# A four-layer graph network on one core: the tie verdict, the refinement loops, the adjacency transfers and the order of the diffusions

## The reference, cut to what matters

```python
def _top_p_attention(X, W1, W2, W3):
    q = X @ W1.T @ W2.T
    k = X @ W3.T
    probs = softmax(q @ k.T, axis=-1)            # 5000 x 5000
    idx = argsort(-probs, axis=-1)
    sp = take_along_axis(probs, idx, axis=-1)
    keep_sorted = cumsum(sp) - sp < 0.9          # top-p: smallest set with 90% of the mass
    A = probs * mask_of(keep_sorted)
    return A / A.sum(-1)
...
R = (adj + eye(N)); R = R / R.sum(-1)
for n in range(2):
    A = _top_p_attention(Xa, W1, W2, W3)
    Xf = R @ Xf                                  # "diffusion"
    Xa = A @ Xa                                  # "attention"
    Z = Z + Xf @ U1[n].T + Xa @ U2[n].T
```

## Time and profile before

| | |
|---|---|
| Time, median of 3 runs | 6468.54 us (6465.03 to 6469.6) |
| The profiled execution | 6475.32 us |
| Its span, from the first to the last instruction | 6473.6 us |
| VectorE busy | 5090.3 us, 79% |
| TensorE busy (matmul) | 4486.8 us, 69% |
| ScalarE busy | 2199.2 us, 34% |
| Mean DMA rate | 84 GB/s |

### The profile page before, as it was taken

The page is one execution under the profiler, slowest core; times in us unless marked ns, Lnnn a source line. Parts: engine busy times, 40 slices in busy tenths (PEclk is TensorE's granted clock), DMA queues, the critical chain, the costliest instruction groups (busy, mean ns, idle before and its releaser), DMA issues. The chain is left out here.

```text
span 6473.6 us, 79162 instructions
## 1 busy us (share of the span) xinstructions
PE 4486.8 (69%) x27812; PEld 3206.8 (50%) x27812; DVE 5090.3 (79%) x12501; ACT 2199.2 (34%) x3353; POOL 327.7 (5%) x170
## 2 busy tenths in 40 slices
PE   6996688888766435452678978575368888847982
PEld 2443377767656335442567867464222222216982
DVE  5887488888518888888888989895649999994875
ACT  2332567666411111111234444233041222214542
POOL 0000000000020000000001000000002022020000
PEclk9997799999889678777889999787689999978996
DMA  8552000000033112111212222112023333314850
GB/s 199 202 200 92 1 2 2 2 2 1 1 115 123 57 53 108 71 72 55 84 72 88 93 80 83 64 64 34 17 70 101 114 111 107 113 35 164 289 189 16
DMA packets 177849, 541.61 MB, mean 84 GB/s; under 512 B 20204, under 2 KB 62303, under 8 KB 177303
## 3 DMA queue, kind: packets, MB, share of 16 engines
q1 hardware_dynamic: 172246, 531.90, 23.7%
q0 software_dynamic: 5120, 3.97, 0.3%
HBM read 524.17 MB, written 11.56 MB: 83 GB/s over the span
## 5 line engine op out<-in xcount | busy, mean ns | idle before, releaser
L680 PE MATMUL ps<-ident,arena 125*125 125x125 f32 x3200 | 539.3, 302 | 863.9 <-DVEq L1186 863.9
L712 PE MATMUL ps<-arena 125*125 125x129 f32 x6400 | 834.5, 289 | 315.3 <-DMA arena<-in_adj_tiles 306.2
L1488 DVE SCALAR_TENSOR_TENSOR arena<-arena,pair 125x1000 f32<-125x1000 f32 x800 | 939.3, 1250 | 69.9 <-ACT arena L1451 69.9
L712 PEld LDWEIGHTS ps<-arena 125*125 125x125 f32 x6400 | 782.3, 199 | 387.1 <-DMA arena<-in_adj_tiles 302.5
L688 PE MATMUL ps<-arena,turned 125*125 125x129 f32 x6400 | 912.3, 290 | 8.0 <-ACT turned L794 8.0
L680 PEld LDWEIGHTS ps<-ident,arena 125*125 125x125 f32 x3200 | 469.5, 215 | 903.8 <-DVEq L1186 903.7
L1506 PE MATMUL ps<-arena 125*64 125x500 f32 x3200 | 763.4, 600 | 194.4 <-DVE arena L1488 194.4
L794 ACT ACTIVATE turned<-ps 125x500 f32<-125x500 f32 x800 | 465.3, 585 | 1268.9 <-PE ps L680 1268.5
L688 PEld LDWEIGHTS ps<-arena,turned 125*125 125x125 f32 x6400 | 838.7, 202 | 19.8 <-ACT turned L794 13.3
L1506 PEld LDWEIGHTS ps<-arena 125*64 125x64 f32 x3200 | 197.4, 137 | 757.4 <-DVE arena L1488 527.3
L1139 DVE SCALAR_TENSOR_TENSOR arena<-arena,wt 125x5000 f32<-125x5000 f32 x80 | 434.1, 5426 | 155.6 <-issue 155.6
(11 more groups left out here) (349 smaller groups left out, 6048.9 us busy)
## 6 DMA issues: line engine op xcount, KB each, us to landing
arena<-in_adj_wide SPq DMA_DIRECT2D x400, 500.0 KB, 4.5
arena<-in_adj_tiles SPq DMA_DIRECT2D x400, 488.3 KB
arena<-in_adj_wide SPq DMA_DIRECT2D x100, 1000.0 KB, 4.7
x_saved<-arena SPq DMA_DIRECT2D x2, 2240.0 KB
arena<-x_saved SPq DMA_DIRECT2D x2, 2240.0 KB
arena<-att_saved SPq DMA_DIRECT2D x1, 2257.5 KB
arena<-in_x SPq DMA_DIRECT2D x1, 2240.0 KB
arena<-in_h SPq DMA_DIRECT2D x1, 2240.0 KB
```

What stands on the lines that cost most here:

```text
L680: mm = pe.transpose(banks_turn[:, g % 2, c * P:(c + 1) * P], work[b % depth][:, j:j + P], ident[0:P, 0:P])
L712: mm = pe.matmul(acc_spread, ring[:, j * P:(j + 1) * P], values[:, j, :], start=(j == 0), stop=False)
L1488: v.scalar_tensor_tensor(out=weight(m).rearrange("p (g w) -> p g w", g=2), in0=rows(ERB + h * N + r * PASS, PASS).rearrange("p (g w) -> p ...
```

## The change

Four things are changed. (a) In `keep`, the drain ahead of the verdict's load goes away; a drain stands inside the branch that needs it. (b) In `refine` both bisection loops are unrolled. (c) In `opened` the nested loops of 4 and 3 rounds give way to one `refine` without a condition, a second under a condition, and under one more a loop of ten; the three are each emitted, so that `opened` holds `refine` three times with its bisections unrolled. (d) The adjacency tiles are laid out with 128 rows for each block, the last three zero, and the ring takes 128 partitions. The order of the diffusions is another: 8, 8, 6, 6, 4, 0, 6, 6 in the first eight blocks, then one in each of 28 blocks, then none. With it `scaled_at` goes from block 9 to block 6.

```diff
-REFINE_ROUNDS = (4, 3)
+REFINE_ROUNDS = 12
-SPREADS = (5, 3, [4] * 8 + [0, 3, 3] + [1, 1, 2, 1] * 6 + [2, 2, 0, 0, 0])
+SPREADS = (5, 3, [8, 8, 6, 6, 4, 0, 6, 6] + [1] * 28 + [0] * 4)
...
-                ring = rows(RING, N)
+                ring, padded_ring = rows(RING, N), rows(RING, N, 128)
...
-                            sp.dma_start(ring[:, q * 1000:(q + 1) * 1000],
-                                         adj_tiles[r * P:(r + 1) * P, q * 1000:(q + 1) * 1000])\
+                            sp.dma_start(padded_ring[:, q * 1000:(q + 1) * 1000],
+                                         adj_tiles[r * 128:(r + 1) * 128, q * 1000:(q + 1) * 1000])\
                               .then_inc(loaded[q], 16)
...
                     def refine(w, cand):
-                        with v.Fori(0, BISECTIONS):
+                        for _ in range(BISECTIONS):
                             bisect(w, dump, goal)
...
-                        with v.Fori(0, CANDIDATE_BISECTIONS):
+                        for _ in range(CANDIDATE_BISECTIONS):
                             bisect(cand, windows, rest)
...
                         v.scalar_tensor_tensor(out=w, in0=w, scalar=found, in1=w, op0=ALU.is_ge, op1=ALU.mult,
                                                accum_out=kept_mass)
-                        v.drain()
                         if rounds > 1:
+                            v.drain()
                             v.match_replace(w, needles[:, 0:8], w, 0.0)
-                            v.drain()
                         ties = worst()
                         with v.If(ties > 0):
+                            v.drain()
                             at = 8 if rounds > 1 else 0
                             v.match_replace(w, needles[:, at:at + 8], w, 0.0)
...
                             mass_above(cand, windows, hi, base)
-                            with v.Fori(0, REFINE_ROUNDS[0]):
-                                second = worst()
-                                with v.If(second > 2):
-                                    with v.Fori(0, REFINE_ROUNDS[1]):
+                            refine(w, cand)
+                            second = worst()
+                            with v.If(second > 2):
+                                refine(w, cand)
+                                third_time = worst()
+                                with v.If(third_time > 2):
+                                    with v.Fori(0, REFINE_ROUNDS - 2):
                                         more = worst()
                                         with v.If(more > 2):
                                             refine(w, cand)
...
-    tiles = adj.reshape(NB, P, NB, P).transpose(0, 3, 2, 1).reshape(N, N)
+    tiles = _np.zeros((NB, 128, NB, P), _np.float32)
+    tiles[:, 0:P] = adj.reshape(NB, P, NB, P).transpose(0, 3, 2, 1)
+    tiles = tiles.reshape(NB * 128, N)
```

## The result

The changed kernel takes 6265.35 us (median of 4 runs, 6259.39 to 6271.09). The kernel before took 6468.99 on the same chip (4 runs, 6465.03 to 6469.6). The ratio is 0.9686, with a 95% interval of 0.967 to 0.9703: 203.6 us less, where 173 were forecast. The profiled execution took 6271.09 us, its span is 6269.3 us.

The account below looks back on a forecast made before the run. VectorE's own sequencer was taken to bound both steps. Terms of 65.5 + 42.5 + 29 + 33 + 6 - 3 = 173 us off 6468.5 gave 6295.5, say 6296 us; range 6264 to 6356 for 8 in 10 and a little more.

Parts of the forecast that it names:

- What bounds the kernel: Both steps: VectorE hardly waits for other engines, so each microsecond of its sequencer in `keep`, `opened` and `refine` counts fully.
- The verdict's load: In `keep`: without the drain, load and branch run under the pass, saving 65.5 us over s0 and s1.
- the load waits for the pass: Rival, in `keep`: the load is held until the pass ends, 57 us are missing, 6353 us; chance 0.06.
- The loops: In `opened` and `refine`, s1: straight code removes waits at loop entries, back edges and exits, saving 42.5 us.
- The way out of `opened`: After a settling refinement: one load and branch with a 3.5 us late jump replace 6.92 us; 11 exits save 29 us.
- In a hinted block that is opened the stall of rows 12 stays.: Hinted opened blocks of s1: an instruction-page stall, 5.11 us for one page under adjacency traffic, remains.
- The transfers: Adjacency tiles: 128 rows use 16 DMA engines, not 5; a diffusion takes 11 us, not 18.9, bounds 9.7 and 13.
- the padded transfer is not faster: Rival: transfers stay at 18.9 us, TensorE needs 39 us in 28 late blocks, some 56 us lost, 6391; chance 0.04.
- The start of s1: Faster diffusions end before the scatters, so the first logits come 33 us earlier, bounds 20 and 38.
- The wait for ScalarE: In s1: pairs of diffusions made VectorE's 7.8 us wait; with the new order 6 us of it go away.
- Fetching in s0: Moved code changes which jumps are late in s0: 3 us lost, bounds 16 gained and 14 lost.
- The jump over `opened`: Rival: the hint no longer brings the target in time, jumps in s0 and s1 become late, 6439 to 6520; chance 0.06.

Follow-up runs that it names:

- e1: Kernel before with only the drain ahead of the verdict's load in `keep` moved into the branch: 6406.49 us against 6472.78, ratio 0.9899.
- e2: Kernel before with only the straight code: bisections unrolled, `opened` with three copies of `refine`: 6406.27 us, ratio 0.99.
- e4: Kernel before with only the new order of the diffusions, tiles of 125 rows: 6457.04 us, ratio 0.9978.
- e3: Kernel before with only the 128-row adjacency tiles, order of the diffusions as before: 6414.56 us, ratio 0.9908.
- e12: Changed kernel with second and later refinements as one compact loop, bisections looped too, save in blocks 1 and 2; 6249.79 us, ratio 0.9663 to the kernel before.
- e7: Changed kernel without any branch prefetch hints: 6399.05 us, ratio 0.9895 to the kernel before.
- e11: Changed kernel with the hint of s0's steps placed ahead of the preceding `keep`, for 11 steps of 12: 6252.66 us, ratio 0.9663 to the kernel before.
- e10: Changed kernel with a hint for the way out of `opened`, inside the first `refine`, in s1's first nine steps: 6250.8 us, ratio 0.9664 to the kernel before.
- e6: Changed kernel with the branch prefetch hint in the first nine steps of s1 too: 6279.6 us, ratio 0.9705 to the kernel before.
- e9: Kernel before, 125-row tiles, with three diffusions ahead of the first logits and five ahead of block 0, not five and three: 6428.63 us against 6468.19, ratio 0.9942.
- e8: Changed kernel with two copies of `refine` in `opened`, the second looped for all later refinements: 6287.01 us against 6470.06, ratio 0.9721.

## Why the prediction was right, point by point

- **What bounds the kernel.** Right. VectorE sets both steps before and after, and the time taken from its sequencer came back in full. From the first step of s1 on TensorE waits on no transfer, and 863.5 us for VectorE.
- **The verdict's load, 65.5 us.** Right: 66.3 alone (e1); in the whole, 30.1 in s1 and 38.7 in s0, of which e1 alone has 36.8. The rival that the load waits for the pass is refuted by the load's start at 1118.4. The reading that the start at 1104.9 beside a running reduction would hold for a pass of 5.4 us was right. The forecast of 0.6 us ahead of L1166 in s0 came true as well.
- **The loops, 42.5 us.** A little high. The eleven blocks gained 87.3. Of it 44.5 stand ahead of L1139 and 5.0 are the stall of the earlier trace rows in block 10, so 37.8 are left for the loops, 2.9 for each refinement. The sum had a slip too: 0.06 us over 78 times is 4.7 us and not 6.2, which would have made it some 44.
- **The way out of `opened`, 29 us: mis-sized, by the hinted blocks.** The wait ahead of L1139 fell by 44.5. The nine blocks without a hint gave 23.5 us of it where 9 x 2.67 = 24 were forecast. That hit is in part luck: a late jump there costs 2.9 us in eight of nine and not 3.5, but block 0 pays 4.86, and behind a second refinement (blocks 1 and 2) the old loops had cost 5.6 and not 6.92. The reason that I gave for a price near the cheap row, idle queues at the end of a refined block, held in eight of nine. The hinted blocks 10 and 33 gave 20.3 us where 5.3 were forecast, and these 15 us are the miss: they leave in 1.30 us or less, with no stall, and the stalls of 6.1 and 3.0 us that the loops' own branches had there went away too. e2 shows that 3.5 would have been too low with the old transfers (5.5 to 6.3 in six of nine blocks); the two edits help each other, which the sum didn't hold.
- **"In a hinted block that is opened the stall of rows 12 stays."** Wrong for block 10, where it went (5.0 us), right for block 33 (2.7 us).
- **The transfers.** Right: five diffusions take 50.3 us (1766.59 to 1816.87), 10.1 each, between my 9.7 and 11, and the share is 0.71. The rule of the Trainium skill cited in the prediction ("DMA: Bandwidth & Descriptors", "Why a DMA increments its semaphore by 16 and not by 1") agrees with this trace as well: more than five engines' worth, where it gives 16 for 128 rows. But the rival that the padded transfer is not faster was priced wrongly: by it the new order with slow tiles would cost 56 us in the late blocks, and e4, which is just that, is 15.7 us faster than before. I had added the 18.9 us of a transfer to TensorE's 20, and they overlap.
- **The start of s1, 33 us: measured 42.0.** Moved as forecast, with the bound going over to the scatters. My chain from the end of the last scatter to the first logits was 9.1 us (1865.3 to 1874.4); it took 4.9 (1825.68 to 1830.63). The last scatter itself starts 139.6 us after s0's last `keep`, where it was 142.7: the pause ahead of it is 2.77 us and not 5.53. And the 1.9 us that I took off for the clock were 0.4 (7.61 us for the first logits against 7.17). These are 8.8 of the 9.
- **The wait for ScalarE, 6 us.** Measured 6.0. I put it down to the pairs of diffusions; e4 takes them away and e3 keeps them with faster tiles, and either alone is enough.
- **Fetching in s0, -3 us.** Zero: seven late jumps before and seven after. My bound of 16 us gained was of the right size: s0 of e12 is 13.4 us shorter than that of the whole change. The back edge gave 5.2 us that I had left out; 128 rows alone gave 3.2 of them (e3).
- **The jump over `opened`.** It did not come true, and e7 shows its size if it had: 134 us, just below the 143 to 224 that I gave. The jumps of s1 cost there no more than those of s0, 65.2 us where I gave 67 to 148.

The forecast's sum was 30.6 us short: 9 at the start of s1, 15.5 at the exits, 5 for block 10's stall, 5.2 at the back edge and 6.9 in s0 (38.7 where I had 34.8 less 3), less 4.7 in the loops, 0.6 in s1's `keep` and 5.5 in the rest of the program. Of the 41.6 us on the plus side 25.7 are the fetching of instructions, which I had counted at one price, and for the hinted blocks as if nothing would change.

## What to carry to other kernels

Where an engine's own sequencer is what the others wait for, load a flag while a long instruction runs and put the drain only into the branch that needs it: 0.8 to 0.9 us for each use here. Price a jump to code that is not there by the transfers that run beside it (2.9 us with quiet queues, 5.5 to 6.3 beside tiles of 125 rows, for the same jump), and give it a hint at a place behind which the code in sequence needs no other fetch: by the stages of the traces a hint moved (e11) or added for the way out (e10) was worth 13 and 12 us more than the whole change, and at the start of blocks that refine hints lost 13 (e6). Before making a transfer faster, look whether fewer of them ahead of the critical work do the same: e9 had the whole gain at the start of s1 for two digits.

## What was not expected of the hardware

- The same jump out of `opened` takes 2.9 to 3.0 us with quiet queues, in the whole change and in e2 alike, and 5.5 to 6.3 beside transfers of 125 rows (e2). Beside transfers of 128 rows it was seen in block 0 alone: 4.86 us in the whole change, 4.50 in e7, although these move more bytes in a second, 270 GB/s against 122 to 127. Why the slower transfers delay a fetch more is open.
- A hint has a price: with it the page that follows in sequence comes late, as stalls of 1.9 to 4.5 us (e6).
- Edits that leave what s0 executes as it is change which of its jumps are late. s0 is 52.1 us shorter than before in e12 and 45.1 in e8, against 38.7 in the whole change; in e8 a part comes back as waits of 14.9 us ahead of L903. Which placement is a good one is open.
- Why block 5 stays late in e10 is open too. e10 and e11 touch different stages and were not run together, so that their sum is not shown.
